# One even spread for every filler of a full batch of an attention and feed-forward layer

## The chip, the cores and the metric

The kernel runs on one core of a Trainium2 chip. The metric is the device time of one execution in microseconds (us), from the profiler, as the median of several runs. The core has a matrix engine (TensorE, PE in the profile, with its weight loads as PEld), VectorE (DVE), ScalarE (ACT), GpSimd (POOL) and SyncE (SP), which here only issues DMAs. Each engine works through its own instructions in order and waits on semaphores for the others.

## The reference, cut to what matters

Sixteen batches of 1024 tokens of width 256 go through one layer: attention with 16 heads of 16, a residual and a layer norm, then a gated feed-forward part of width 768 with its own residual and norm.

```python
q = split_heads(x @ Wq.T + bq); k = ...; v = ...
scores = einsum('hbnd,hbmd->hbnm', k, q) / 16
out = merge_heads(softmax(scores) @ v) @ Wo.T + bo
x = layernorm(x + out)
h = silu(x @ wg.T) * (x @ wu.T)          # wg, wu, wd: integers / 127
x = layernorm(x + h @ wd.T)
```

## The kernel before, in words

**Steps.** A batch is cut into 64 steps (STEPS): 4 groups of 4 heads, 2 halves of 512 query columns, 8 tiles of 128 key rows. In a step PE computes four score matmuls (`score`), two halves of two, each half into two PSUM banks. ScalarE takes the exponential of each half (L608, 128x1024, twice a step) into `probs`. At every even step PE also does the 16 product matmuls with v of the two steps before (`products`), which add up in one bank for 8 steps, a segment. VectorE then transposes the segment out of PSUM (`take_segment`, L877) and scales it by the sums of the exponentials (`scale_segment`, L885 to L896; four of the segments, 2, 3, 6 and 7, are scaled the long way, with a second transpose, a cast and a subtraction).

**Fillers.** At every odd step PE does other matrix work instead of products, the fillers. For batch b these are the projections of batch b + 1 (`qk` 0 to 7, `norm` 0 and 1, `v` 0 to 3) and what follows the attention of batch b - 1 (`out` 0 to 3, `x1T` 0 to 3, which transposes, `gate` and `up` 0 to 11, `down` 0 to 3). COST gives for each kind the number of its pieces (a matmul or so) and the ns of one; by it all fillers of a full batch take 54.2 us of matrix time. Every filler goes to one of three PSUM banks in turn (RINGS = 3): filler n waits until filler n - 3 is drained (`ring_free`). A bank is drained by VectorE, for a qk or gate after ScalarE's part: a copy of the high half (L580), or the tanh (L589). For an up, VectorE multiplies (L789) and casts (L793), and GpSimd subtracts (L517).

**Blocks and plans.** A list of 32 blocks says which pieces each odd step holds. `evenly` cuts a list of fillers into blocks of equal cost at piece borders, so that a filler may go over two blocks. `Plan` takes the blocks and gives each item of the other engines' work a date in steps: ScalarE's part half a step after the block in which the filler ends if it ends within SOON (1250 ns) of the block's start, else one and a half; VectorE's drain one step or so after it; GpSimd's behind that. VectorE's and GpSimd's orders are their items sorted by date. Into VectorE's order go also the segments (`take` at 8s + 0.55, `scale` at 8s + 1.3) and, after the drain of v 3, the two halves of `scale_x` (L799 and L801), at 0.3 and 0.7 behind v 3's date. `scale_x` makes the scaled fp16 input for the batch after next. GpSimd's maximum over x is put ahead of its first item dated 12.2 or later.

**The flag.** Ahead of step 58 (RELOAD) PE waits for `flag_ready`. VectorE sets it in `decide` (L828, L831), which its program runs ahead of its first item dated 58 or later, so behind the scaling of segment 6 (dated 57.3). The flag says whether the next batch needs the careful softmax, with a maximum per row; with this input it never does, and `prepare_shift` only clears a tile (L871).

**Which batches.** Batches 1 to 14 run FULL_PLAN. Batch 0 runs PRE_PLAN, without the work behind an attention, and batch 15 POST_PLAN, without projections.

Of the kernel before, what the change touches and what calls it, by code (L numbers as in the profile page):

```python
# [23 lines left out]
HCHUNKS = HIDDEN // P  # L24
# [40 lines left out]
STEPS = GROUPS * HALVES * TILES  # L65
# [12 lines left out]
def some(kind, *js):  # L78
    return [(kind, j) for j in js]


def gate_up(*gs):
    return [(kind, g) for g in gs for kind in ("gate", "up")]


def evenly(items, steps):

    total = sum(COST[kind][0] * COST[kind][1] for kind, _ in items)
    blocks = [[] for _ in range(steps // 2)]
    at = 0  # L90
    for kind, j in items:
        count, cost = COST[kind]
        where = [min(steps // 2 - 1, (at + cost * i + cost // 2) * (steps // 2) // total) for i in range(count)]
        at += count * cost
        for m in sorted(set(where)):
            blocks[m].append((kind, j, where.index(m), count - where[::-1].index(m)))
    return blocks

FULL_BLOCKS = (evenly(some("qk", 0, 1, 2, 3) + some("out", 0, 1, 2, 3)
                      + [item for j in range(4) for item in some("x1T", j) + some("qk", 4 + j)], 20)  # L100
               + [some("norm", *{3: (0,), 5: (1,)}.get(g, ())) + gate_up(g) for g in range(2 * HCHUNKS)]
               + evenly(some("v", 0, 1) + some("down", 0) + some("v", 2, 3) + some("down", 1, 2, 3), 20))
FULL = list(dict.fromkeys((kind, j) for block in FULL_BLOCKS for kind, j, *_ in block))


# [88 lines left out]
PREPARES = [PER_GROUP * g + PREPARE for g in range(GROUPS - 1)] + [STEPS - 4]  # L194
FULL_PLAN, PRE_PLAN, POST_PLAN = Plan(FULL_BLOCKS, PREPARES), Plan(evenly(ONLY_PRE, PRE_STEPS), PREPARES), Plan(POST_BLOCKS, PREPARES[:-1])
LOADS = 4 * len(Q_PARTS)
# [1098 lines left out]
```

## Time and profile before

| what | us |
|---|---|
| median of 3 runs | 2596.5 (2596.32 to 2596.59) |
| the profiled execution | 2599.36 |
| its span, first to last instruction | 2597.3 |
| PE busy | 2475.1 (95%) |
| ScalarE busy | 2131.6 (82%) |
| VectorE busy | 1399.3 (54%) |
| GpSimd busy | 539.6 (21%) |
| start of batches 6 and 7 (first exponential) | 989.00 and 1142.95 |

The span is the time between the first and the last instruction of the profiled execution; its whole time is 2.1 us longer. A row of a timeline gives start, length, engine, line, instruction and how often it came in a row; in brackets stands how long the engine was idle before it, and who released it. Rows of PE and PEld overlap, since matmuls are pipelined. All fillers and scores share one line, so PE's rows are told apart by the tiles' names: `kstack,qstack` are scores, `probs,v` products, `Wv,x` a v, `ffn,gateT` a gate, `ffn,upT` an up, `downT,ffn` a down, `squares,heads` a norm.

### The profile page before, as it was taken

To read this page: it belongs to the slowest core of one execution; us is meant where nothing else is said; L and a number is where in the kernel's file an instruction comes from. 1 tells how busy PE (TensorE), PEld (TensorE's weight loads), DVE (VectorE), ACT (ScalarE), POOL (GpSimd) and SP (SyncE) were. 2 spreads that over 40 slices of the span, in tenths; PEclk is the share of its full clock that TensorE was granted. 3 is DMA by queue.
4 is the path that set the end of the run, shared out by engine and by line. 5 is a ranking of instruction groups with operands and counts; after the bars stand their busy time and mean duration, and the time that the engine had idled before them with its cause. 6 is when DMAs were issued, how large, how long until landed. Compare 5 with 4: busy or idle time off the path is not lost. (4 is left out here: it accounts for less than half of the span.)

```text
span 2597.3 us, 48910 instructions
## 1 busy us (share of the span) xinstructions
PE 2475.1 (95%) x18062; PEld 883.9 (34%) x18062; DVE 1399.3 (54%) x3008; ACT 2131.6 (82%) x2370; POOL 539.6 (21%) x542
## 2 busy tenths in 40 slices
PE   4878999999999999999999999999999999998996
PEld 2222243333333333333333323333333333333333
DVE  5334546464654655556464654645565465553547
ACT  1887988888898888888888898888889888887881
POOL 2101212122220312212131221212222131221113
PEclk9998999999999999999999999999999999999998
DMA  4112121030211212121030212103121120211100
GB/s 144 46 42 73 33 74 59 14 107 26 79 42 36 85 26 91 32 89 43 22 99 26 90 32 74 60 14 107 27 79 42 38 84 26 91 33 56 26 18 33
DMA packets 81750, 144.20 MB, mean 56 GB/s; under 512 B 27584, under 2 KB 29504, under 8 KB 79424
## 3 DMA queue, kind: packets, MB, share of 16 engines
q1 hardware_dynamic: 79968, 139.81, 17.2%
q8 instruction: 178, 2.92, 0.5%
q14 instruction: 100, 0.82, 0.1%
q10 hardware_dynamic: 1504, 0.66, 0.1%
HBM read 88.48 MB, written 50.33 MB: 53 GB/s over the span
## 5 line engine op out<-in xcount | busy, mean ns | idle before, releaser
L608 ACT ACTIVATE probs<-psum 128x1024 f32<-128x1024 f32 x2048 | 1984.3, 1024 | 366.6 <-PE psum L1046 366.4
L1046 PE MATMUL psum<-probs,v 128*32 128x512 f32 x8192 | 996.7, 604 | 0.8 <-ACT probs L608 0.8
L1046 PE MATMUL psum<-kstack,qstack 51*128 51x512 f16 x4096 | 635.2, 384 | 67.6 <-ACT probs L608 30.4
L1046 PEld LDWEIGHTS psum<-kstack,qstack 51*128 51x128 f16 x4096 | 147.0, 93 | 710.6 <-ACT probs L608 598.7
L1046 PEld LDWEIGHTS psum<-probs,v 128*32 128x32 f32 x8192 | 214.7, 109 | 489.6 <-issue 485.9
L517 POOL TENSOR_TENSOR ffn<-h,ffn 128x512 f16<-128x512 f32 x192 | 222.0, 1156 | 676.0 <-DVE ffn L793 676.0
L747 DVE SCALAR_TENSOR_TENSOR tanh_out<-tanh_out,psum 128x512 f32<-128x512 f32 x192 | 131.6, 686 | 287.1 <-ACT tanh_out L589 287.1
L510 POOL TENSOR_TENSOR rstd<-vareps,minus_half 128x2 f32<-128x2 f32 x128 | 91.1, 712 | 760.9 <-DVE vareps L815 760.9
L738 DVE SCALAR_TENSOR_TENSOR parts<-psum,scales,parts 128x512 f16<-128x512 f32 x128 | 95.3, 745 | 200.1 <-ACT parts L580 199.9
L1046 PE MATMUL psum<-ffn,gateT 128*128 128x512 f16 x768 | 199.8, 383 | 0.3 <-DVE ffn L781 0.3
L1046 PE MATMUL psum<-ffn,upT 128*128 128x512 f16 x768 | 197.7, 380 | 0.4
L1046 PE MATMUL psum<-downT,ffn 128*128 128x256 bf16 x1536 | 189.1, 274 | 0.0
L877 DVE STREAM_TRANSPOSE flipped<-psum 128x512 f32<-128x512 f32 x128 | 91.6, 716 | 180.5 <-PE psum L1046 180.4
L496 POOL TENSOR_TENSOR squares<-parts 128x512 bf16<-128x512 f16 x128 | 130.8, 1044 | 227.8 <-DVE parts L738 162.1
L1046 PEld LDWEIGHTS psum<-downT,ffn 128*128 128x128 f16 x1536 | 141.8, 98 | 61.1 <-issue 45.5
L789 DVE SCALAR_TENSOR_TENSOR h<-tanh_out,h_scale,psum 128x512 f32<-128x512 f32 x192 | 143.5, 747 | 18.5 <-DVE tanh_out L747 0.5
L589 ACT ACTIVATE tanh_out<-psum 128x512 f32<-128x512 f32 x192 | 116.3, 606 | 41.7 <-PE psum L1046 41.7
L773 DVE SCALAR_TENSOR_TENSOR x_res<-psum,down_scale,x_res 128x512 f32<-128x512 f32 x64 | 47.9, 748 | 159.4 <-PE psum L1046 159.4
L822 DVE TENSOR_SCALAR x_res<-x_res,meanvar,rstd 128x256 f32<-128x256 f32 x256 | 93.6, 408 | 67.5 <-POOL rstd L510 67.4
L580 ACT ACTIVATE parts<-psum,scales 128x512 f16<-128x512 f32 x128 | 88.9, 695 | 32.0 <-PE psum L1046 24.5
L530 POOL TENSOR_TENSOR x_res<-x_res,bo_all 128x2048 f32<-128x2048 f32 x16 | 72.6, 4536 | 182.1 <-DMA x_res<-in_L_attn_x 182.1
L761 DVE COPY v<-psum 128x512 f32<-128x512 f32 x64 | 44.2, 690 | 122.5 <-PE psum L1046 122.5
(120 smaller groups left out, 1645.1 us busy)
## 6 DMA issues: line engine op xcount, KB each, us to landing
parts_dram<-parts SPq DMA_DIRECT2D x64, 512.0 KB, 2.9
qstack<-parts_dram SPq DMA_DIRECT2D x384, 64.0 KB, 2.1
kstack<-parts_dram SPq DMA_DIRECT2D x384, 64.0 KB, 2.1
x_pre<-in_x_t SPq DMA_DIRECT2D x17, 1024.0 KB, 7.7
x_res<-in_L_attn_x SPq DMA_DIRECT2D x16, 1024.0 KB, 4.8
out<-x_res SPq DMA_DIRECT2D x32, 512.0 KB, 2.7
kstack<-shift_parts SPq DMA_DIRECT2D x384, 4.0 KB, 1.7
ffn<-in_L_ffn_w_gate SPq DMA_DIRECT2D x1, 768.0 KB, 7.0
```

The source lines that it names most:

```text
L496: nc.gpsimd.tensor_tensor(squares[:, idx, cols], parts[:, idx % 2, 0, cols], parts[:, idx % 2, 0, cols], ALU.mult).then_inc(squares_ready, 1)
L510: nc.gpsimd.tensor_tensor(rstd[:, tiles], vareps[:, tiles], minus_half[:, tiles], ALU.pow).then_inc(rstd_ready, 1)
L517: nc.gpsimd.tensor_tensor(hT[hf][1][:, hc, :], h32[:, g % 2, :], hT[hf][0][:, hc, :], ALU.subtract).then_inc(h_lo_ready, 1)
L580: nc.scalar.activation(parts[:, idx % 2, 0, hf * HALF:(hf + 1) * HALF], bank[RING + (start + n) % RINGS], ACT.Identity, bias=scales[:, par ...
L589: nc.scalar.activation(tanh_out[:, g % 2, :], bank[RING + (start + n) % RINGS], ACT.Tanh, scale=0.5 * W_SCALE).then_inc(tanh_ready, 1)
L608: nc.scalar.activation(probs[:, (STEPS * b + k) % SLOTS, 2 * pr:2 * pr + 2, :], scores[pr], ACT.Exp, scale=score_scale[par]).then_inc(prob ...
L738: nc.vector.scalar_tensor_tensor(out=parts[:, idx % 2, 1, cols], in0=o, scalar=scale[:, BIAS + idx:BIAS + idx + 1], in1=parts[:, idx % 2, ...
L747: nc.vector.scalar_tensor_tensor(out=gated, in0=gated, scalar=1.0, in1=o, op0=ALU.add, op1=ALU.mult).then_inc(ring_free, 1)
L789: nc.vector.scalar_tensor_tensor(out=h32[:, j % 2, :], in0=tanh_out[:, j % 2, :], scalar=h_scale[:, 0:1], in1=o, op0=ALU.mult, op1=ALU.mul ...
L822: ins = nc.vector.tensor_scalar(x_res[:, t, :], x_res[:, t, :], meanvar[:, t, 0:1], rstd[:, t:t + 1], ALU.subtract, ALU.mult)
L877: nc.vector.transpose(flipped[:, hf, :], bank[ACC]).then_inc(acc_free, 1)
L1046: return nc.tensor.matmul(o, lhsT, rhs, start=start, stop=stop)
```

## The change

One list of fillers is spread by `evenly` over all 32 blocks of a full batch. Before, the first 10 blocks (qk, out, x1T) and the last 10 (v, down) were spread each for themselves, and between them stood 12 blocks with a whole gate and a whole up each, two of these with a norm besides. The order of the fillers stays; COST, the dates' rules and all other plans too.

```diff
-FULL_BLOCKS = (evenly(some("qk", 0, 1, 2, 3) + some("out", 0, 1, 2, 3)
-                      + [item for j in range(4) for item in some("x1T", j) + some("qk", 4 + j)], 20)
-               + [some("norm", *{3: (0,), 5: (1,)}.get(g, ())) + gate_up(g) for g in range(2 * HCHUNKS)]
-               + evenly(some("v", 0, 1) + some("down", 0) + some("v", 2, 3) + some("down", 1, 2, 3), 20))
+FULL_BLOCKS = evenly(some("qk", 0, 1, 2, 3) + some("out", 0, 1, 2, 3)
+                     + [item for j in range(4) for item in some("x1T", j) + some("qk", 4 + j)]
+                     + [item for g in range(2 * HCHUNKS)
+                        for item in some("norm", *{3: (0,), 5: (1,)}.get(g, ())) + gate_up(g)]
+                     + some("v", 0, 1) + some("down", 0) + some("v", 2, 3) + some("down", 1, 2, 3), STEPS)
```

Worked out from the two lists, the loads of the odd steps by COST, in ns:

| odd steps | before | after |
|---|---|---|
| 1 to 11 | 1728 each | 1728, 1728, 1728, 1620, 1620, 1728 |
| 13 to 19 | 1732 each | 1732, 1732, 1732, 1516 |
| 21 to 43 | 1728, in 27 and 31 2058 | 1728, in 27 and 31 1626 |
| 45 to 53 | 1512, 1620, 1512, 1620, 1512 | 1620, 1620, 1728, 1728, 1728 |
| 55 to 63 | 1512, 1620, 1512, 1620, 1512 | 1620, 1728, 1728, 1620, 1728 |

Gates 0 to 4 then end over 1250 ns into their block and get their tanh one step later than before. v 3 ends in step 55 instead of 53. In the changed kernel all lines behind the list are one higher.

VectorE ahead of the flag, in a full batch, from the drain of v 3 on (`v`); `x` is the scaled input, `flipped` the segment. Before:

```order
L761 COPY v<-psum 128x16x2x16 x2
L799 TENSOR_SCALAR x<-x_pre,scales 128x2x512
L801 SCALAR_TENSOR_TENSOR x<-x_pre,scales,x 128x2x512
L799 TENSOR_SCALAR x<-x_pre,scales 128x2x512
L801 SCALAR_TENSOR_TENSOR x<-x_pre,scales,x 128x2x512
L877 STREAM_TRANSPOSE flipped<-psum 128x512
L885 RECIPROCAL inv<-flipped 128x16
L887 TENSOR_TENSOR scaled<-flipped,inv 128x16x16
```

And now:

```order
L762 COPY v<-psum 128x16x2x16 x2
L800 TENSOR_SCALAR x<-x_pre,scales 128x2x512
L802 SCALAR_TENSOR_TENSOR x<-x_pre,scales,x 128x2x512
L878 STREAM_TRANSPOSE flipped<-psum 128x512
L800 TENSOR_SCALAR x<-x_pre,scales 128x2x512
L802 SCALAR_TENSOR_TENSOR x<-x_pre,scales,x 128x2x512
L886 RECIPROCAL inv<-flipped 128x16
L888 TENSOR_TENSOR scaled<-flipped,inv 128x16x16
```

The second half of the input scaling went from ahead of the segment's transpose to behind it, ahead of the segment's scaling. The copy's "x2" is v 2 and v 3.

PE in steps 25 to 29 of a full batch, around norm 0. Before:

```order
L1046 MATMUL psum<-ffn,gateT 128x512 x4
L1046 MATMUL psum<-ffn,upT 128x512 x4
L1046 MATMUL psum<-kstack,qstack 128x512 x4
L1046 MATMUL psum<-probs,v 32x512 x8
L1046 MATMUL psum<-kstack,qstack 128x512 x4
L1046 MATMUL psum<-squares,heads 32x512 x4
L1046 MATMUL psum<-ffn,gateT 128x512 x4
L1046 MATMUL psum<-ffn,upT 128x512 x4
```

And now:

```order
L1047 MATMUL psum<-ffn,upT 128x512 x2
L1047 MATMUL psum<-ffn,gateT 128x512 x4
L1047 MATMUL psum<-ffn,upT 128x512 x2
L1047 MATMUL psum<-kstack,qstack 128x512 x4
L1047 MATMUL psum<-probs,v 32x512 x8
L1047 MATMUL psum<-kstack,qstack 128x512 x4
L1047 MATMUL psum<-ffn,upT 128x512 x2
L1047 MATMUL psum<-squares,heads 32x512 x4
L1047 MATMUL psum<-ffn,gateT 128x512 x4
```

Step 25 held gate 2 and up 2, and now holds the second half of up 1, gate 2 and the first half of up 2; step 27 held norm 0, gate 3 and up 3, and now the rest of up 2, norm 0 and gate 3.

VectorE behind segment 2 (the last two rows of its scaling stand first), where `tanh_out` is the drain of a gate and `h` that of an up. Before:

```order
L894 CAST out<-flipped 128x512
L896 TENSOR_TENSOR out<-flipped,out 128x512
L747 SCALAR_TENSOR_TENSOR tanh_out<-tanh_out,psum 128x512
L789 SCALAR_TENSOR_TENSOR h<-tanh_out,h_scale,psum 128x512
L793 CAST ffn<-h 128x512
L753 TENSOR_REDUCE norms<-psum 128x1
```

And now:

```order
L895 CAST out<-flipped 128x512
L897 TENSOR_TENSOR out<-flipped,out 128x512
L790 SCALAR_TENSOR_TENSOR h<-tanh_out,h_scale,psum 128x512
L794 CAST ffn<-h 128x512
L748 SCALAR_TENSOR_TENSOR tanh_out<-tanh_out,psum 128x512
L790 SCALAR_TENSOR_TENSOR h<-tanh_out,h_scale,psum 128x512
```

Up 1 now stands behind segment 2 and ahead of gate 2; gate 1 went from ahead of the transpose to between transpose and scaling.

## Rows read from the trace of the kernel before

**Rows 1.** The page: busy time, share of the span, and instructions of each engine.
```profile
PE 2475.1 (95%) x18062; PEld 883.9 (34%) x18062; DVE 1399.3 (54%) x3008; ACT 2131.6 (82%) x2370; POOL 539.6 (21%) x542
```

**Rows 2.** Waits of PE: us in total, times, longest.
```profile
PE psum L1046 <- DVE flag L831: 30.3, 15, 3.6
```

**Rows 3.** Timeline of ScalarE, starts of steps 24, 26, 28: start, length, what, idle before.
```profile
1046.45 1.94 ACT L608 ACTIVATE probs<-psum 128x1024 f32<-128x1024 f32 x2
...
1051.21 1.94 ACT L608 ACTIVATE probs<-psum 128x1024 f32<-128x1024 f32 x2
...
1056.30 1.02 ACT L608 ACTIVATE probs<-psum 128x1024 f32<-128x1024 f32 x1 [0.27 <-PE psum L1046]
```

**Rows 4.** Timeline of ScalarE, steps 46, 47, 48 and 50.
```profile
1099.31 1.94 ACT L608 ACTIVATE probs<-psum 128x1024 f32<-128x1024 f32 x2 [0.23 <-PE psum L1046]
...
1101.73 1.94 ACT L608 ACTIVATE probs<-psum 128x1024 f32<-128x1024 f32 x2 [0.49 <-PE psum L1046]
...
1104.01 1.94 ACT L608 ACTIVATE probs<-psum 128x1024 f32<-128x1024 f32 x2 [0.34 <-PE psum L1046]
...
1108.58 1.02 ACT L608 ACTIVATE probs<-psum 128x1024 f32<-128x1024 f32 x1 [0.23 <-PE psum L1046]
```

**Rows 5.** Timeline, steps 53 to 60: what leads to the flag and follows it.
```profile
1115.79 1.70 PE L1046 MATMUL psum<-Wv,x 128*128 128x256 f16 x14
...
1117.53 0.69 DVE L761 COPY v<-psum 128x512 f32<-128x512 f32 x1 [0.62 <-PE psum L1046]
...
1118.14 0.74 DVE L799 TENSOR_SCALAR x<-x_pre,scales 128x1024 f16<-128x1024 f32 x1
...
1120.16 0.75 DVE L799 TENSOR_SCALAR x<-x_pre,scales 128x1024 f16<-128x1024 f32 x1
...
1122.45 1.94 ACT L608 ACTIVATE probs<-psum 128x1024 f32<-128x1024 f32 x2 [0.23 <-PE psum L1046]
...
1124.59 0.72 DVE L877 STREAM_TRANSPOSE flipped<-psum 128x512 f32<-128x512 f32 x1 [2.33 <-PE psum L1046]
...
1128.68 0.61 PE L1046 MATMUL psum<-kstack,qstack 51*128 51x512 f16 x4 [1.88 <-DVE flag L831]
...
1129.22 1.92 PE L1046 MATMUL psum<-probs,v 128*32 128x512 f32 x16
...
1131.61 1.70 PE L1046 MATMUL psum<-downT,ffn 128*128 128x256 bf16 x14
```

**Rows 6.** Timeline of VectorE from segment 2's transpose to norm 0, steps 24 to 27.
```profile
1048.54 0.72 DVE L877 STREAM_TRANSPOSE flipped<-psum 128x512 f32<-128x512 f32 x1
...
1052.27 0.68 DVE L747 SCALAR_TENSOR_TENSOR tanh_out<-tanh_out,psum 128x512 f32<-128x512 f32 x1
...
1054.23 0.68 DVE L753 TENSOR_REDUCE norms<-psum 128x1 f32<-128x512 f32 x1
```

**Rows 7.** Timeline of GpSimd: the maximum over x.
```profile
1028.91 0.38 POOL L488 PARTITION_ALL_REDUCE xmax_all<-xmax_safe  x1 [6.03 <-issue]
```

**Rows 8.** Windows of 6.4 us behind flag waits: busy times, granted clock (PEclk), DMA.
```profile
665.30:671.70 6.40, 6.40 (x54) 2.52 (x58) 2.88 (x10) 5.31 (x6) 0.69 (x1) 1.00 0.01 1
819.30:825.70 6.40, 6.40 (x42) 2.17 (x42) 2.83 (x10) 3.88 (x4) 0.69 (x1) 0.73 0.01 3
```

**Rows 9.** Timeline of PE: batch 0's flag wait, batch 1's start, batch 4's flag wait.
```profile
195.46 0.61 PE L1046 MATMUL psum<-kstack,qstack 51*128 51x512 f16 x4 [3.62 <-DVE flag L831]
195.99 3.61 PE L1046 MATMUL psum<-probs,v 128*32 128x512 f32 x16
...
214.73 1.04 PE L1046 MATMUL psum<-kstack,qstack 51*128 51x512 f16 x4 [3.95 <-issue]
...
220.11 1.90 PE L1046 MATMUL psum<-x,Wq 128*128 128x512 f16 x8
...
819.75 2.80 PE L1046 MATMUL psum<-probs,v 128*32 128x512 f32 x16
...
825.91 0.64 PE L1046 MATMUL psum<-probs,v 128*32 128x512 f32 x4
```

## Prediction

> **What bounds the kernel now.** I read the page first: TensorE (PE) is busy 95% of the span and ScalarE (ACT) 82% [rows 1]. The list of who waits for whom has one wait that PE meets once a batch: for VectorE's flag, 30.3 us in 15 waits of up to 3.6 us [rows 2]. So in a full batch PE is the bound, save one wait.
>
> The timeline of ScalarE gives the length of every pair of steps, since each step starts with two exponentials. A pair with a gate and an up (COST 1728) lasts 1051.21 - 1046.45 = 4.76 us; with a norm (2058) 1056.30 - 1051.21 = 5.09 us. The difference is 0.33 us, all of the norm's 330 ns [rows 3]. At the light end, 1108.58 - 1104.01 = 4.57 us for 1512, 0.19 less for 216 ns less filler [rows 4]. Time is thus linear in filler over the range that the change evens out: PE pays each filler once, wherever it stands. Both plans hold the same 54.2 us of fillers by COST. Evening out as such saves nearly nothing, and what counts is which waits come and go.
>
> The one wait is the flag. In the batch that starts at 989.00 the transpose of segment 6 starts at 1124.59, since the products before it end only then (VectorE had idled 2.33 us). Behind it, in VectorE's fixed order, stand the scaling, decide and the flag; PE resumes at 1128.68 after 1.88 us without work [rows 5]. That is a chain of 4.09 us from the transpose's start. It is the same in all 14 full batches, and sets the time there.
>
> **The change, part by part.**
>
> *1. The second input scaling moves behind the transpose.* v 3 used to end with step 53 and now ends six matmuls into step 55. The planner dates both halves of scale_x behind it, at 56.3 and 56.7, and segment 6 at 56.55: the second half lands between transpose and scaling. Before, both stand ahead of the transpose, which then waited 2.33 us for PE. Where they will now stand: the filler of step 55 starts 0.11 after its exponentials, six matmuls at 108 ns are 0.65, the copy of v starts about 0.23 after the end of its matmuls (fourteen from 1115.79, copy at 1117.53), and scaling starts 0.61 after the copy. So the first half starts 1.60 us into step 55, takes 2.02 (1118.14 to 1120.16) and ends 3.62 in. Step 55, now 1620, lasts 2.28 (1104.01 - 1101.73 for the same load [rows 4]); it ends 1.34 into step 56, and the transpose starts 2.14 into step 56 (1124.59 - 1122.45). The first half is hidden with 0.8 us to spare. The second adds its full 2.02, and about 0.01 for a drain: **+2.03 us**. Nothing covers it, as PE already stands. Queued behind it are decide, the drain of down 1 and y 1; PE, then ScalarE, wait for the flag.
>
> *2. Work hidden in that wait.* Step 57 holds 16 down matmuls instead of 15: **-0.11 us**, since one more runs before the wait. The stall becomes 1.88 + 2.03 - 0.11 + 0.04 (step 57 starts a little earlier without the light step 55), 3.84 us.
>
> *3. Light steps.* After a 1512 step PE's second score pair waits for the exponential of the step before: the step behind a 1512 lasts 1101.73 - 1099.31 = 2.42 [rows 4], where otherwise products to fillers are 1131.61 - 1129.22 = 2.39 [rows 5]. I count 0.04 for each of five, rounding up, less 0.04 for the new light step 19 (1516): **-0.16 us**.
>
> *4. The gates split over blocks.* A gate that ends past 1250 ns in its block gets its tanh one step later (gates 0 to 4), so its bank comes free later, and PE comes back to banks in the middle of a block. I go through them by rows. Tanh follows the step's two exponentials (1.94 [rows 3]) and takes about 0.6, so VectorE can start a gate 2.5 into the step and ends it 0.68 later [rows 6]. For up 1, wanted 1.4 us into step 23, gate 0 is free at about 0.8: no wait. The tight one is gate 3 in step 27. It needs gate 2 drained. VectorE runs from transpose start to gate 2 in 3.73 us now, and a round of gate, up and cast takes 1054.23 - 1052.27 = 1.96 [rows 6]. The new order puts one such round in between, as gate 1 behind the transpose and up 1 behind the scaling. From step 24's start: transpose 2.09 (1048.54 - 1046.45), gate 2 at 2.09 + 3.73 + 1.96 = 7.78, free 0.75 later with 0.07 for the signal, at 8.53. PE wants it at 4.76 + 2.39 + 0.10 + 0.43 + 0.33 = 8.01, so it waits 0.52 at most; a gate with a clear behind it instead of its up overlaps more, by some 0.1. **+0.40 us**. From gate 5 on tanh is in its own step again, and nothing waits.
>
> *5. VectorE, GpSimd and the queues otherwise.* The maximum over x now stands ahead of out 3 in GpSimd's order, not behind. It occupies 6.4 us, of which 6.03 without an instruction [rows 7]. Out 3's rstd then comes at about 1.7 us into step 15 and its norm on VectorE ends by 2.5, when qk 4's drain can start at the earliest: nothing. Squares of qk 4 to 7 come a step later, and SyncE's stores and the shift loads queued behind them too; the stack that they fill is wanted seven steps on. Down 3 ends the batch on both sides, so the boundary keeps its shape. I cost these at zero; if a cover is gone, 0.4 us a batch, the size of gate 3's wait.
>
> Sum by batch: 2.03 - 0.11 - 0.16 + 0.40 = 2.16 us, times 14 full batches **+30.2 us**. Batches 0 and 15 have plans of their own.
>
> *6. The clock.* A longer stall also touches PE's clock. In the 14 stalls of 1.88 us the granted clock stayed 1.00 in the window after the stall eleven times, and fell thrice to 0.73 on the mean [rows 8]; after those PE ran at 1.2 GHz for a while. Sixteen product matmuls took 2.80 us instead of 1.92 [rows 5, 9], and from products to products 825.91 - 819.75 = 6.16 us instead of the 4.57 of a pair with that load [rows 4, 9]: 1.59 us each. The nearest rows to a 3.84 us stall are two outside the full batches: after 3.62 us of stall the products took 3.61 instead of 1.92, so 1.69; after 3.95 us 220.11 - 214.73 = 5.38 instead of 1131.61 - 1128.68 = 2.93, so 2.45 [rows 5, 9]. Bounds by batch: nothing more than now, and 2.45. I take 1.69, the nearest, in all 14, less what is paid already: 14 x 1.69 - 3 x 1.59 = **+18.9 us**. The ends are 0 and 14 x 2.45 - 4.8 = +29.5.
>
> By the Trainium skill (TensorE: Matmul & The Clock Gate, Part 1) the penalty is the throttled time times one minus the granted ratio, so a clock penalty ends at half the throttled time. The window of [rows 8] at 0.73 over 6.40 us is 3.46 us at half rate, 1.73 us by that rule against the 1.59 read off; by it the clock term is 14 x 1.73 - 3 x 1.73 = 19.0, an estimate hardly other than the sum's.
>
> The profiled execution took 2599.36 us (span 2597.3), 2.9 over the median of 2596.5. The sum on it is 2599.4 + 49.1 = 2648.5, on the median **2645.6**.
>
> **The rivals.**
> *Late flag, steady clock.* The stall grows as above, but the clock falls no oftener than now. For: eleven of fourteen stalls left it alone. Against: both stalls above 3.6 us were followed by 1.2 GHz. 2596.5 + 30.2 = 2626.7.
> *VectorE is ahead of my reckoning.* Then the second scaling fits ahead of the transpose and gate 2 is drained in time. It decides at v 3's end: it would have to be 1.2 us earlier (3.62 + 2.02 - 2.28 - 2.14). Then points 2 and 3 give -0.27 x 14 = -3.8, and a stall of 1.8 us that no longer drops the clock gives -4.8: 2587.9, faster. Against: the order on VectorE is fixed, the scaling stands behind the transpose.
> *VectorE backs up.* More bank waits than gate 3's around segment 2, where VectorE goes from segment 2 straight to gate 2 and norm 0 [rows 6]: twice 0.4 us more by batch and the upper clock bound, 2596.5 + 30.2 + 11.2 + 29.5 = 2667.
> *Nothing happens.* Loads were 1512 to 2058 and are 1516 to 1732; with PE the bound and the scaling hidden by something I miss, 2596.5.
>
> **How the numbers follow.** Forecast 0.70, late flag with steady clock 0.13, VectorE backs up 0.08, nothing 0.05, faster 0.04. Range: the low end is the steady-clock case with the gate wait gone, 2596.5 + 14 x 1.76 = 2621; the high end the forecast with the upper clock bound and one more wait of 0.4, 2596.5 + 30.2 + 29.5 + 5.6 = 2662. Some 0.17 lies outside. Within 0.2%, about what a measurement can tell here, is 2591.3 to 2601.7: 0.05; faster 0.04; slower 0.91.
>
> **What would show it.** VectorE's timeline near step 56: transpose, then a pair of scaling instructions, then the reciprocal. PE's wait for the flag: 14 of about 3.8 us, some 57 us in all with batch 0's. PE resumes 8.3 us after step 56's exponentials instead of 1128.68 - 1122.45 = 6.23 [rows 5]. Granted clock below 1.00 in the window after nearly every stall. One wait of about 0.4 us for a tanh_out drain in step 27. The second norm's pair at 4.66 instead of 5.09, the first's near 5.0, and pairs of the last third at 4.66 to 4.77. I am wrong if the stall stays 1.9 us, or if the products behind it take 1.92.

## The result, and the profile after

| | median, us | runs | lowest to highest |
|---|---|---|---|
| before | 2596.55 | 4 | 2596.32 to 2598.03 |
| after | 2780.31 | 4 | 2778.86 to 2781.14 |

The ratio is 1.0706, with a 95% interval of 1.0687 to 1.0724: 184 us slower, where 49 were forecast. The direction was right and the size wrong; the time lies 118 us over the range's high end. The profiled execution of the changed kernel took 2781.14 us, its span is 2779.1.

The page's first part (engine, busy us, share of the span, instructions), against [rows 1]:

```profile
PE 2538.8 (91%) x18062; PEld 892.7 (32%) x18062; DVE 1392.0 (50%) x3008; ACT 2132.2 (77%) x2370; POOL 541.0 (19%) x542
```

The same instructions, and but for PE the same busy times. PE is 64 us busier with an equal count of matmuls, since the clock granted to it was lower (0.954 on the mean of the span, 0.987 before), and it idles more. What it waits for, us in total, times, longest, against [rows 2]:

```profile
PE psum L1050 <- DVE parts L739: 89.9, 14, 6.9
PE psum L1047 <- DVE flag L832: 56.6, 15, 4.0
```

The second row is the wait that the prediction had put at some 57 us. The first row did not exist before, and no step of the prediction has it: 14 waits, one a full batch, of 6.4 us each, in which a transpose (L1050) waits for the drain of a qk (`parts`). By the starts of ScalarE's exponentials, the mean batch of the 14 grew by 12.8 us. Worked out from these starts by pairs of steps: pairs 16 and 18 together +9.5, pair 56 +1.95, pair 58 +1.50, all the rest -0.1.

The place in the batch that starts at 1055.02, rows from the timelines of all engines, steps 13 to 18. `rstd` is the reciprocal of the standard deviation, which the layer norm behind an out needs; GpSimd makes it from `vareps`, the variance, and VectorE scales the tile with it (L823).

```profile
1085.65 0.69 POOL L511 TENSOR_TENSOR rstd<-vareps,minus_half 128x2 f32<-128x2 f32 x1 [2.92 <-DVE vareps L816]
...
1086.30 0.19 POOL L487 TENSOR_TENSOR xmax_safe<-xmax,margin 128x1 f32<-128x1 f32 x1
...
1089.01 0.17 DVE L816 TENSOR_SCALAR vareps<-meanvar 128x2 f32<-128x2 f32 x1
...
1090.60 1.94 ACT L609 ACTIVATE probs<-psum 128x1024 f32<-128x1024 f32 x2 [0.45 <-PE psum L1047]
...
1092.43 0.69 ACT L581 ACTIVATE parts<-psum,scales 128x512 f16<-128x512 f32 x1
...
1092.89 0.38 POOL L489 PARTITION_ALL_REDUCE xmax_all<-xmax_safe  x1 [6.40 <-issue]
...
1100.60 0.73 POOL L511 TENSOR_TENSOR rstd<-vareps,minus_half 128x2 f32<-128x2 f32 x1 [7.33 <-issue]
1101.37 0.73 DVE L823 TENSOR_SCALAR x_res<-x_res,meanvar,rstd 128x256 f32<-128x256 f32 x2 [10.83 <-POOL rstd L511]
1102.02 0.74 DVE L739 SCALAR_TENSOR_TENSOR parts<-psum,scales,parts 128x512 f16<-128x512 f32 x1
...
1102.82 1.12 PE L1050 MATMUL psum<-ident,x_res 128*128 128x128 f32 x4 [6.95 <-DVE parts L739]
...
1107.08 1.94 ACT L609 ACTIVATE probs<-psum 128x1024 f32<-128x1024 f32 x2 [9.19 <-PE psum L1047]
```

Read it from below. PE's transposes of x1T 2 waited 6.95 us for the bank of qk 4. ScalarE had done its part of qk 4 by 1093.12, but VectorE drained it only at 1102.02, because its order has out 3's norm ahead and it stood 10.83 us for GpSimd's rstd. The variance for that rstd was there at 1089.18. GpSimd did nothing with it for 11.4 us: it had begun the maximum over x at 1086.30, idled 6.40 us before the cross-partition instruction (line L489, 0.38 us) and, which is new to a reader of [rows 7], 7.33 us behind it with nothing to wait for ("issue"). Together they take GpSimd from 1086.30 to 1100.60, 14.3 us. Behind the stall the four transposes took 1.12 us, where they took 0.66 before, so the clock was low too: 0.58 in the 6.4 us from 1102.8 on, and 0.51 to 0.61 in the like windows of all 14 batches.

Why the maximum moved: out 3 now ends in step 13 instead of 11, which dates its rstd 14.0 instead of 12.0, and the maximum goes ahead of the first item dated 12.2 (POOL_XMAX) or later.

The flag's place in the same batch, against [rows 5]:

```profile
1198.11 1.28 DVE L802 SCALAR_TENSOR_TENSOR x<-x_pre,scales,x 128x1024 f16<-128x1024 f32 x1
1200.08 0.72 DVE L878 STREAM_TRANSPOSE flipped<-psum 128x512 f32<-128x512 f32 x1 [0.69 <-PE psum L1047]
1200.72 0.71 DVE L800 TENSOR_SCALAR x<-x_pre,scales 128x1024 f16<-128x1024 f32 x1
1201.51 1.28 DVE L802 SCALAR_TENSOR_TENSOR x<-x_pre,scales,x 128x1024 f16<-128x1024 f32 x1
1202.89 0.25 DVE L886 RECIPROCAL inv<-flipped 128x16 f32<-128x16 f32 x1
...
1206.17 0.61 PE L1047 MATMUL psum<-kstack,qstack 51*128 51x512 f16 x4 [3.76 <-DVE flag L832]
1206.70 3.23 PE L1047 MATMUL psum<-probs,v 128*32 128x512 f32 x16
```

As forecast: first half of the scaling hidden (0.69 us of idle left ahead of the transpose, 0.8 forecast), the second half between transpose and reciprocal, a stall of 3.76 us (3.84 forecast), and products of 3.23 us instead of 1.92 behind it.

### The profile page after: what moved, and what is told of

It is laid out like the page before. It is cut to its first block and busy times, and to the rows that moved or that the text cites. A ratio compares the mean times of both kernels' runs of the same rounds, so it can differ in the third digit from the quotient of the medians.

```text
span 2779.1 us, 48910 instructions
## 1 busy us (share of the span) xinstructions
PE 2538.8 (91%) x18062; PEld 892.7 (32%) x18062; DVE 1392.0 (50%) x3008; ACT 2132.2 (77%) x2370; POOL 541.0 (19%) x542
## 5 line engine op out<-in xcount | busy, mean ns | idle before, releaser
L1047 PE MATMUL psum<-probs,v 128*32 128x512 f32 x8192 | 1021.5, 617 | 0.8 <-ACT probs L609 0.8
L1047 PE MATMUL psum<-kstack,qstack 51*128 51x512 f16 x4096 | 644.9, 390 | 90.0 <-DVE flag L832 56.6
L511 POOL TENSOR_TENSOR rstd<-vareps,minus_half 128x2 f32<-128x2 f32 x128 | 90.4, 706 | 826.0 <-DVE vareps L816 632.5
L1047 PE MATMUL psum<-ffn,gateT 128*128 128x512 f16 x768 | 215.3, 382 | 2.7 <-DVE tanh_out L748 1.0
L823 DVE TENSOR_SCALAR x_res<-x_res,meanvar,rstd 128x256 f32<-128x256 f32 x256 | 93.5, 407 | 239.7 <-POOL rstd L511 239.7
L1047 PE MATMUL psum<-ffn,upT 128*128 128x512 f16 x768 | 205.2, 381 | 0.4
L1050 PE MATMUL psum<-ident,x_res 128*128 128x128 f32 x256 | 47.1, 318 | 96.0 <-DVE parts L739 89.9
L1047 PE MATMUL psum<-x,Wk 128*128 128x512 f16 x384 | 115.5, 430 | 9.7 <-DVE parts L739 6.3
```

Source lines behind the costliest of these rows:

```text
L511: nc.gpsimd.tensor_tensor(rstd[:, tiles], vareps[:, tiles], minus_half[:, tiles], ALU.pow).then_inc(rstd_ready, 1)
L823: ins = nc.vector.tensor_scalar(x_res[:, t, :], x_res[:, t, :], meanvar[:, t, 0:1], rstd[:, t:t + 1], ALU.subtract, ALU.mult)
L1047: return nc.tensor.matmul(o, lhsT, rhs, start=start, stop=stop)
```

## The experiments

Each kernel was timed beside the kernel before on the same chip, where that took 2596.9 to 2598.7 us, and ratios are to it. Theory G: the maximum over x, moved ahead of out 3's rstd on GpSimd, makes the unforeseen 9.5 us a batch. Rival B: PE waits for qk 4's bank because the change split qk 4 over two blocks and drains it a step later, as the wait's own row names that drain.

### The move on GpSimd, undone and done alone

```diff
# x1_max_behind_out3, on the changed kernel
-POOL_XMAX, POOL_NORMS = 12.2, 48.9
+POOL_XMAX, POOL_NORMS = 14.1, 48.9
```

> The changed kernel with GpSimd's maximum over x put back behind out 3's rstd (dated 14.1 instead of 12.2), nothing else. Theory G (the cross-partition reduction and the 7.3 us that follow it hold up out 3's rstd, VectorE behind it, and PE's bank in step 17): pair 16 falls from 13.55 to about 4.8 us and pair 18 from 5.57 to 4.8, so 14 x 9.5 = 133 us go and about 2647 us are left, near what the prediction's sum said. Rival B (PE's wait for qk 4's drain in step 17 comes from the split of qk 4 over two blocks and its later drain): no change, 2780 us.

Measured: 2647.7 us, ratio 1.0185 (1.0166 to 1.0204). The wait for `parts` in step 17 is gone; out 3's rstd is made first:

```profile
1042.73 0.69 POOL L511 TENSOR_TENSOR rstd<-vareps,minus_half 128x2 f32<-128x2 f32 x1 [2.92 <-DVE vareps L816]
...
1049.77 0.38 POOL L489 PARTITION_ALL_REDUCE xmax_all<-xmax_safe  x1 [6.20 <-issue]
1057.59 3.03 POOL L497 TENSOR_TENSOR squares<-parts 128x512 bf16<-128x512 f16 x3 [7.44 <-DVE ffn L782]
```

This one number takes back 132.6 us, and what is left is within 2.1 us of the prediction's 2645.6. qk 4 is still split, so rival B falls.

```diff
# x2_before_max_ahead, on the kernel before
-if at >= POOL_XMAX and not scaled:
+if (at >= POOL_XMAX or not first and (kind, j) == ("out", 3)) and not scaled:
```

> The kernel before with one thing of the change alone: GpSimd's maximum over x stands ahead of out 3's rstd. Theory G: rstd of out 3 comes some 14 us after out 2's, VectorE stands as long, x1T 0's bank is not free when qk 5 wants it in step 15, and PE stalls about 13 us a batch: about 2596 + 182 + some 20 us for the clock = 2800 us. Rival B: nothing moves, 2596 us.

Measured: 2800.8 us, ratio 1.0775 (1.0747 to 1.0802). In the old layout of blocks the same move costs even more than in the new one, since x1T 0's drain stands behind out 3's norm there, and its bank is wanted in step 15. PE's row and the wait's total:

```profile
1111.93 2.74 PE L1046 MATMUL psum<-x,Wq 128*128 128x512 f16 x6 [11.42 <-DVE ffn L781]
```
```profile
PE psum L1046 <- DVE ffn L781: 164.0, 15, 12.3
```

One move on GpSimd alone makes the slowdown, without any of the spreading.

```diff
# x7_even_plain_max, on the changed kernel
-nc.gpsimd.partition_all_reduce(xmax_all[:, :], xmax_safe[:, :], P, RMAX).then_inc(xmax_reduced, 1)
+nc.gpsimd.tensor_tensor(xmax_all[:, :], xmax_safe[:, :], margin[:, 0:1], ALU.mult).then_inc(xmax_reduced, 1)
```

> The changed kernel with its order, but GpSimd's cross-partition maximum over x is replaced by a plain multiplication of the same tile; the scale of x is then each partition's own, and the result another. Theory G in its narrow form (it is the cross-partition instruction with what is loaded before and after it that costs 14 us of GpSimd's time): out 3's rstd comes in time, pair 16 at 4.8 us, 2648 us. Rival (any work between out 2's and out 3's rstd holds GpSimd up, by its queue): pair 16 stays above 10 us, 2750 us or more.

Measured: 2647.8 us, ratio 1.0192 (1.0172 to 1.0213). The order is the changed kernel's, maximum first, and it costs nothing now:

```profile
1038.90 0.19 POOL L487 TENSOR_TENSOR xmax_safe<-xmax,margin 128x1 f32<-128x1 f32 x1
1039.24 0.20 POOL L489 TENSOR_TENSOR xmax_all<-xmax_safe,margin 128x1 f32<-128x1 f32 x1
1041.86 0.69 POOL L511 TENSOR_TENSOR rstd<-vareps,minus_half 128x2 f32<-128x2 f32 x1 [2.42 <-DVE vareps L816]
```

With a plain instruction in its place there is no idle time before it, and behind it only VectorE's 2.42 us. So both gaps, 6.4 us ahead and 7.3 us behind, belong to the cross-partition instruction, not to the place in the queue.

The Trainium skill has the first of the two (GPSIMD Engine Reference, 2.1 Instruction dispatch): kernels of GpSimd can be loaded while the program runs, and the first call to one freshly loaded costs about 6 us, with no row of its own in the profile. The trace agrees in size (6.03 in [rows 7], 6.40 and 6.20 above). For the second, the way back to ordinary instructions, the trace has one more hint. GpSimd's sequencer runs instructions named MODIFY_POOL_CONFIG, of 0.01 and 0.08 us: two ahead of each reduction, and two more behind it, on the line of whatever comes next. The changed kernel's rows by line (instruction, how many, shortest, median and longest in ns, first and last start), and then x7's, which has none left on L489 and half as many on L511:

```profile
L489 POOLq MODIFY_POOL_CONFIG  x32: 11/11/11, 48.3 to 2424.7; - x32
L511 POOLq MODIFY_POOL_CONFIG  x56: 82/83/83, 257.5 to 2522.2; - x56
```
```profile
L511 POOLq MODIFY_POOL_CONFIG  x28: 82/83/83, 337.6 to 2391.3; - x28
```

The 56 are two for each of the 28 reductions of the full batches, since each of these batches has a second one, over the norms. So the same instruction stands in both gaps and goes with both. That the time of the second gap is spent on loading is inferred from this, not shown.

### The late scaling alone

```diff
# x3_before_scale_late, on the kernel before, in Plan
-dve += [(max(at, SCALE + 1.0) + 0.3 + 0.4 * hf, "xT", hf, n) for hf in range(HALVES)]
+dve += [(56.7 if hf and 53 < at < 55 else max(at, SCALE + 1.0) + 0.3 + 0.4 * hf, "xT", hf, n) for hf in range(HALVES)]
```

> The kernel before with the second half of the input scaling behind segment 6's transpose in full batches, as the change has it, and nothing else. Prediction's terms 1 and 6: flag stall 1.88 -> 3.9 us, 14 x 2.03 = 28 us, and the clock falls after each of the 14 stalls, 14 x 1.69 - 3 x 1.59 = 19 us: 2644 us. Rival (steady clock, or the clock's fall lies in the stall): 2625 us.

Measured: 2648.3 us, ratio 1.0190 (1.0170 to 1.0209), 50 us more than before where 47 were expected. PE's waits for the flag, and one stall with the slow products behind it:

```profile
PE psum L1046 <- DVE flag L831: 58.2, 15, 4.1
```
```profile
1148.67 1.03 PE L1046 MATMUL psum<-kstack,qstack 51*128 51x512 f16 x4 [3.87 <-DVE flag L831]
1149.63 3.07 PE L1046 MATMUL psum<-probs,v 128*32 128x512 f32 x16
```

The flag's total grew from 30.3 to 58.2, 27.9 us for 14 batches, 1.99 each. The other 22 us are the clock. In all 14 windows of 6.4 us behind a stall the granted clock is below 1.00, in ten of them between 0.73 and 0.76, in one 0.78, and in three 0.54 or 0.55. One window of the first kind and one of the last (columns: window, length, busy time of each engine, granted clock, DMA):

```profile
359.50:365.90 6.40, 6.40 (x40) 2.21 (x40) 2.90 (x10) 3.83 (x4) 0.69 (x1) 0.73 0.01 3
...
675.00:681.40 6.40, 6.40 (x32) 1.65 (x29) 2.65 (x9) 3.41 (x4) 0.70 (x1) 0.54 0.01 2
```

Worked out for these 14 batches, pairs 56 and 58 grew by 3.53 us on the mean, of which 1.99 are stall and 1.54 clock on top of what three falls had cost.

### The flag made early

```diff
# x4_before_decide_early, on the kernel before
-DECIDE, RELOAD = 57, 58
+DECIDE, RELOAD = 53, 58
```

> The kernel before with decide at step 53 instead of 57, so that it does not stand behind segment 6's scaling. If the flag wait is the one wait of a full batch and costs what its rows say: 14 x 1.88 + 3.6 us of stall and 3 x 1.59 + 1.69 us of slow clock go, -36 us: 2560 us. Rival (PE would next wait for something else in step 58, such as the products' bank): -10 us or less, 2587 us or more.

Measured: 2565.3 us, ratio 0.9874 (0.9852 to 0.9896), 33 us less than before where 36 were expected. No wait for the flag is left, and pair 56 lasts 4.71 us. A batch is now the same to 0.01 us from the third on, as the starts of batches 6 and 7 show one case of:

```profile
974.95 1.94 ACT L608 ACTIVATE probs<-psum 128x1024 f32<-128x1024 f32 x2 [0.23 <-PE psum L1046]
...
1127.03 1.94 ACT L608 ACTIVATE probs<-psum 128x1024 f32<-128x1024 f32 x2 [0.23 <-PE psum L1046]
```

From start to start that is 152.08 us, against 153.95 before and 155.5 in batches with a slow stretch.

x8_scale_late_decide_early is the kernel before with x3's and x4's edits both.

> The kernel before with both of x3's and x4's edits: the second half of the input scaling behind segment 6's transpose, and decide at step 53. If the scaling costs only by standing ahead of the flag, its 2.03 us are now hidden: 2565 us, as x4. Rival (VectorE's later work is late in any case, and PE waits for a bank in steps 59 to 63): up to 14 x 2 us more, 2593 us.

Measured: 2565.0 us, ratio 0.9877 (0.9861 to 0.9893), x4's time. VectorE's timeline has the same late scaling between transpose and reciprocal, but the flag was made long before:

```profile
1102.05 0.16 DVE L831 TENSOR_TENSOR flag<-over 128x1 int32<-128x1 f32 x1
...
1110.73 0.72 DVE L877 STREAM_TRANSPOSE flipped<-psum 128x512 f32<-128x512 f32 x1 [4.35 <-PE psum L1046]
1111.38 0.71 DVE L799 TENSOR_SCALAR x<-x_pre,scales 128x1024 f16<-128x1024 f32 x1
1112.16 1.28 DVE L801 SCALAR_TENSOR_TENSOR x<-x_pre,scales,x 128x1024 f16<-128x1024 f32 x1
1113.54 0.25 DVE L885 RECIPROCAL inv<-flipped 128x16 f32<-128x16 f32 x1
```

So the late scaling costs only by standing ahead of the flag.

### The even spread with its waits removed

x6_even_two_repairs is the changed kernel with x1's edit and x4's. x5_even_repaired has one more, `SOON = 1300` instead of 1250. x9_even_gates_1_2_early has instead:

```diff
# x9_even_gates_1_2_early, beside x1's and x4's edits
-self.ends[n], self.soon[n] = 2 * m + 1, took <= SOON
+self.ends[n], self.soon[n] = 2 * m + 1, took <= (1300 if (kind, j) in (("gate", 1), ("gate", 2)) else SOON)
```

> As x5_even_repaired but with SOON left at 1250 ns, so gate 3 still waits for gate 2's bank: 4 us more than it, 2564 us; pair 26 at 4.95 us instead of 4.66. Rival (the wait only moves other slack): the same time as x5_even_repaired.

> The changed kernel with three repairs: the maximum over x behind out 3's rstd (14.1), decide at step 53, and SOON at 1300 ns, so that gates 0 to 2 get their tanh in the step in which they end. From x1's 2647.7 us: the flag's stall goes (14 x 3.84 + 3.6 = 57 us), the slow clock after it goes (14 x 1.84 + 1.7 = 27 us), and gate 3's wait goes (14 x 0.29 = 4 us): 2560 us. Against x4's 2565 us it is the even spread as such, which then is worth 14 x (0.11 + 0.16) = 4 us. Rival (an even spread saves as soon as no wait stands in the way, since ScalarE's light and heavy steps balance): 2550 us or less.

> As x6_even_two_repairs, but gates 1 and 2 (not 0) get their tanh in the step in which they end. x5_even_repaired did that for gate 0 too and put two ScalarE items into step 21: pair 20 grew from 4.60 to 5.08 us and ate the gain. Expected: pair 20 back at 4.60, pair 26 at 4.77 instead of 4.96, a batch at 151.9 us instead of 152.08, and 14 x 0.18 = 2.5 us less than x6_even_two_repairs: 2560 us. Rival (gate 3's bank is not what holds pair 26, VectorE's queue in general is, so the wait turns up in another pair): a batch stays at 152.1 us, 2562.5 us.

| | median, us | ratio (95%) | batch 6, us |
|---|---|---|---|
| x4, blocks as before | 2565.3 | 0.9874 (0.9852 to 0.9896) | 152.08 |
| x6, even | 2562.6 | 0.9868 (0.9852 to 0.9885) | 152.07 |
| x5, even, SOON 1300 | 2567.2 | 0.9886 (0.9870 to 0.9903) | 152.22 |
| x9, even, gates 1 and 2 early | 2562.1 | 0.9864 (0.9844 to 0.9884) | 151.89 |

The intervals overlap, so the medians do not order these four. The batches tell more: they are of one profiled execution each, but equal from batch to batch to 0.01 us but for a few. The means of the 14 full batches, of which the first is always longer, are 152.25 (x4), 152.28 (x6), 152.30 (x5) and 152.05 (x9); x6 has two batches of 152.45, in which pair 26 lasted 5.33 us. The starts of x9's batches 6 and 7:

```profile
974.28 1.02 ACT L609 ACTIVATE probs<-psum 128x1024 f32<-128x1024 f32 x1 [0.45 <-PE psum L1047]
...
1126.17 1.02 ACT L609 ACTIVATE probs<-psum 128x1024 f32<-128x1024 f32 x1 [0.45 <-PE psum L1047]
```

x5 missed its expectation of 2560 us, and x6 with it: it was to take 4 us more than x5 and took 4.6 less. Gate 0's tanh then falls into step 21, where ScalarE already has qk 7's high half, so step 22's exponentials start late:

```profile
1026.73 1.94 ACT L609 ACTIVATE probs<-psum 128x1024 f32<-128x1024 f32 x2 [0.26 <-PE psum L1047]
1028.55 0.69 ACT L581 ACTIVATE parts<-psum,scales 128x512 f16<-128x512 f32 x1
1029.12 0.61 ACT L590 ACTIVATE tanh_out<-psum 128x512 f32<-128x512 f32 x1
1029.60 3.84 ACT L609 ACTIVATE probs<-psum 128x1024 f32<-128x1024 f32 x4
```

Pair 20 lasted 5.08 us with it and 4.60 in x6 and x9. x9's pairs and batch came as expected (its median, 0.5 us below x6's instead of 2.5, cannot tell): pair 26 went from 1041.78 - 1036.83 = 4.95 in x6 to 1040.68 - 1035.91 = 4.77, and the batch from 152.07 to 151.89:

```profile
1036.83 1.94 ACT L609 ACTIVATE probs<-psum 128x1024 f32<-128x1024 f32 x2 [0.43 <-PE psum L1047]
...
1041.78 1.02 ACT L609 ACTIVATE probs<-psum 128x1024 f32<-128x1024 f32 x1 [0.62 <-PE psum L1047]
```
```profile
1035.91 1.94 ACT L609 ACTIVATE probs<-psum 128x1024 f32<-128x1024 f32 x2
...
1040.68 1.02 ACT L609 ACTIVATE probs<-psum 128x1024 f32<-128x1024 f32 x1 [0.44 <-PE psum L1047]
```

With the waits for the maximum, the flag and gate 3's bank gone, the even spread is worth 152.08 - 151.89 = 0.19 us a batch, 2.7 us in all, 0.1%: under what these runs can tell on the median. x5's rival of 2550 us or less falls. The best kernels here are x4 and the ones like it, 1.3% faster than before by one number, DECIDE.

## Why the prediction was wrong, step by step

**What bounds the kernel: right in the main.** Time is near linear in filler: in the changed kernel pairs 48 and 52, up by 216 ns by COST, went from 4.57 to 4.78 us. The two pairs with a norm depart from it. Pair 30, down from 2058 to 1626, was to last 4.66 us and lasted 4.77, and so did pair 26 where gate 3 does not wait (x9). A norm there stands behind half an up and starts 0.54 us after it, where COST has 0.43; that takes some 0.2 us a batch of what the spread could save. The spread as such gives nothing (x4 against x6: 152.08 and 152.07).

**Step 1, the scaling behind the transpose: right.** 2.03 us forecast, 2.00 from transpose start to PE's restart (1206.17 - 1200.08 = 6.09, less the 4.09 of before), and 1.99 in x3, where it stands alone. Step 2: the stall was 3.76, 3.84 forecast.

**Step 3, light steps: right in size.** -0.16 forecast for a batch. No run has this term alone; all that the spread does once the waits are gone is -0.19 (x9 against x4).

**Step 4, gate 3's bank: mechanism right, size off.** 0.40 forecast, 0.18 by x6 against x9, or 0.24 on the mean of the 14 batches. The term's PE side was too early: the half up takes 0.54 us until the norm starts (1129.60 - 1129.06), where COST's 0.43 was used. The rest is mostly on VectorE's side: in x6 it began gate 2's drain 7.58 us after step 24's start (1039.64 - 1032.06), where 7.78 was reckoned.

```profile
1129.06 0.60 PE L1047 MATMUL psum<-ffn,upT 128*128 128x512 f16 x2
1129.60 0.40 PE L1047 MATMUL psum<-squares,heads 128*32 128x512 bf16 x4
```

**Step 5, "I cost these at zero": this is what failed.** It said that the maximum over x "occupies 6.4 us" and that out 3's rstd "then comes at about 1.7 us into step 15". It came at 1101.33 - 1090.60 = 10.7. Of the 9 us, 7.33 are the gap behind the cross-partition instruction, which the step did not have; the rest, some 1.7, is that the reduction ended (1093.27) later than reckoned. An estimate from these rows: with the 7.33 alone missing, qk 4's drain would have ended at 1102.76 - 7.33 = 1095.43, 0.4 us before x1T 2 wanted its bank (1102.82 - 6.95 = 1095.87): the step's zero would have held. With the gap, VectorE stood 10.83 us and PE 6.95. The step's fallback, 0.4 us a batch if a cover is gone, was a guess, not the length of what was behind the cover. The rival that VectorE backs up also had PE wait for VectorE's drains, but around segment 2, by VectorE's own work and at 0.4 us each.

The gap was in the trace of before, under another name. GpSimd's next row behind [rows 7], whose reduction ended at 1029.29, is:

```profile
1036.42 3.03 POOL L496 TENSOR_TENSOR squares<-parts 128x512 bf16<-128x512 f16 x3 [7.13 <-DVE parts L738]
```

The 7.13 us are put down to VectorE's drains. But three squares follow without a pause, so the drains for the second and third were not late either, and VectorE's rows have the first drain, qk 4's, ready before the reduction even ran, and the next soon behind it:

```profile
1025.04 0.75 DVE L738 SCALAR_TENSOR_TENSOR parts<-psum,scales,parts 128x512 f16<-128x512 f32 x1 [0.17 <-ACT parts L580]
...
1030.04 0.71 DVE L738 SCALAR_TENSOR_TENSOR parts<-psum,scales,parts 128x512 f16<-128x512 f32 x1
```

GpSimd could have started the first square at 1029.29 and started it at 1036.42. Nobody waited for the squares then, so it cost nothing. The change put an rstd there that VectorE waits for, and PE behind it.

**Step 6, the clock: right.** The forecast of a fall behind each of the 14 stalls held: the changed kernel has a granted clock of 0.73 or 0.74 in all 14 windows. One fall cost 1.64 us in pair 58 (6.43 against 4.57 before plus 0.22 for the heavier step), 1.69 forecast. Where the flag's stall stands without step 17's, in x3, three of fourteen stalls cost a longer slow stretch, and the mean over the fourteen was higher than forecast by 0.2 us. The longer stall of step 17 has a slow clock behind it too, which, with a short wait for x1T 1's drain behind it (0.25 us of `ffn` in the batch above), makes 6.42 us of idle on the mean into the 8.74 by which pair 16 grew, and some of pair 18's 0.75.

The sum without step 5's miss: 14 x 3.33 us measured (12.82 less the 9.49 of pairs 16 and 18) against 14 x 3.51 forecast; and x1, which undoes the miss alone, came out at 2647.7 against 2645.6. That it is so near is in part luck, since two errors cancel in it: gate 3's wait was less than forecast, and the clock behind the flag's stalls cost more (pair 58 lasted 6.61 us on the mean, and 6.41 in the changed kernel).

## What to carry to other kernels

When an item moves in an engine's order, price the whole stretch for which that engine is taken, up to the start of its next instruction, and check the releaser that a trace names for the idle time behind it: several instructions that then run without a pause are a hint, and the rows of the engine named say when the input was really there. An order sorted by dates moves things that no line of the change mentions, so compare all queues, the idle ones first, and ask for each swap who waits for what now comes second. And where one engine pays for every filler wherever it stands, evening out its load gains almost nothing; taking a flag out from behind work that it does not need gained 1.3%.

## What the runs showed of the hardware

A cross-partition reduction on GpSimd of 0.38 us takes that engine for about 14 us, each time that it is called: in the full batches of all traces GpSimd was idle 5.9 to 6.9 us before it, and 6.7 to 7.9 us behind it where the next instruction's inputs were there. With a plain multiplication in its place (x7) both are gone.

TensorE's clock went to 1.2 GHz behind every one of the flag's stalls of 3.8 to 4.1 us (14 of 14 in the changed kernel, in x1 and in x3). Behind stalls of 1.9 to 2.1 us it went there in 3 of 14 before and in 6 of 14 in x2, by a granted clock of 0.73 in the window behind. A fall cost about 1.6 us in most of them, nearly as much as a 1.88 us stall itself, and now and then 2.7: pair 58 lasted up to 7.25 us in x3, where 4.57 is undisturbed.
